# LayerNorm statistics computed on ScalarE instead of VectorE in a fused attention and recurrent-gate kernel

## The chip, the cores and the metric

One Trainium2 chip (trn2), all of its 8 cores, which run the same program on different rows and don't talk to each other. The metric is device time in microseconds (us) of the slowest core; the profile is of that core, here core 5.

## The reference

```python
# x: (8, 4096, 1024) fp32; 16 heads, hd = 64; layernorm over the last axis, eps = 1e-5
def attn(x):
    q, k, v = (x @ W.T).reshape(N, S, H, hd).transpose(0, 2, 1, 3)   # for Wq, Wk, Wv
    att = einsum('nqhd,nkhd->nhqk', q, k)       # q and k run over the 16 heads of one token
    att = softmax(att / sqrt(hd), axis=3)
    return einsum('nhqk,nkhd->nqhd', att, v).reshape(N, S, D) @ Wo.T + bo

def ffn(x):                                     # scan over the first axis, 8 steps
    step: f = sigmoid(xt @ wf.T + c @ uf.T + bf); i = sigmoid(xt @ wi.T + c @ ui.T + bi)
          g = tanh(xt @ wc.T + c @ uc.T + bc);    c = f * c + i * g
    return tanh(x @ wo.T + c_final @ uo.T + bo)

x = x + layernorm(attn(layernorm(x)))
x = x + layernorm(ffn(layernorm(x)))
```

Attention goes over the heads of one token, so a 128x128 score tile packs 8 tokens by 16 heads, and masked rows of qst and kst cut it to its blocks.

## The kernel before

Each core holds 512 tokens of each of the 8 batches. Every engine has one queue in program order, written out by hand; `P("vector", f)` appends f to VectorE's queue, and semaphores in `Chan` objects order the engines. `f_...` are the pieces, named as in the code. SBUF tiles of 128 rows by 1024 columns are double-buffered (`buf`, `zbuf`); the four row statistics s1, s2, mean and rstd have one column for each buffer (`sl`).

**Projection tiles** (from L1486, four for each batch): POOL loads 128 rows of x into xin (`f_load`, L1500), once tile t-2 has been applied. Then come the statistics (`ln_stats`), the apply on VectorE (L1516, xln_sb), 8 transposes on TensorE (L1531), a copy (L1541), 48 matmuls for q, k and v (L1555) with VectorE's evictions (L1570), and transposes of q and k with four strided copies on VectorE into qst and kst (L1618). All of this is one chain; the next tile's row sum stands in VectorE's queue behind the last copy into kst.

**Attention groups** (16 for each batch): POOL loads vst (L1644), TensorE makes the scores (L1660), ScalarE the exp (L1672), TensorE the product with v (L1692), VectorE evicts and normalises (L1708, L1741), SP stores.

**P2** (`emit_P2`, from L1358) is the output projection of the batch before, one row tile after every fourth group: POOL loads zin, TensorE transposes, 16 matmuls (L1421), VectorE adds the bias in two halves (L1432, zb), statistics, then on VectorE apply (L1460) and residual (L1463), and POOL stores x1 (L1472). POOL's queue holds that store ahead of the next loads of vst or xin. The last batch's four row tiles come at the end.

**Stage of transposes** (32 tiles, after a barrier): x1 is loaded into xin (L1858), statistics, apply (L1881), transposes (L1893), copy (L1902), and a spill to xt_scr on SP (L1910). VectorE's first piece waits for the load of the gate weights as well (L1867).

**Scan** (L1969 to L2002): no LayerNorm in it. **Output matmuls** (32 row tiles): POOL loads gat from xt_scr (L2041), two groups of 17 matmuls (L2062, L2069, L2075), ScalarE evicts each through tanh into h (L2084), VectorE sums h and its squares (`f_hstat`, L2094, L2095). **Last stage**: apply and residual on VectorE, loads and stores on POOL.

`ln_stats` (L57) queues on VectorE a row sum (L61), a sum of squares as accumulator of a product (L62), and four operations on one column for mean and variance (L65 to L70); then on ScalarE Ln and Exp for rstd (L76, L78).

Of the kernel before, what the change touches and what calls it, by code (L numbers as in the profile page):

```python
# [9 lines left out]
AF = mybir.ActivationFunctionType  # L10
AL = mybir.AluOpType
AX = mybir.AxisListType.X

D = 1024
# [5 lines left out]
EPS = 1e-5  # L20
# [36 lines left out]
def ln_stats(P, ch_sum, ch_rst, xi, sq_junk, sl, s1, s2, mean, var, msq,  # L57
             rstd, epst, width):
    def f_sums(v, xi=xi, sl=sl):
        v.drain()  # L60
        v.reduce_sum(s1[:, sl], xi, axis=AX)  # L61
        v.scalar_tensor_tensor(sq_junk, xi, 1.0, xi, AL.mult, AL.mult,  # L62
                               accum_out=s2[:, sl])
        v.drain()  # L64
        v.tensor_scalar_mul(mean[:, sl], s1[:, sl], 1.0 / width)  # L65
        v.scalar_tensor_tensor(msq[:, sl], s1[:, sl], 1.0 / (width * width),
                               s1[:, sl], AL.mult, AL.mult)
        v.tensor_scalar_mul(var[:, sl], s2[:, sl], 1.0 / width)
        v.drain()
        ch_sum.inc(v.tensor_sub(var[:, sl], var[:, sl], msq[:, sl]))  # L70
    P("vector", f_sums)
    ch_sum.bump()

    def f_rstd(sc, sl=sl, sm=ch_sum.n):
        sc.wait_ge(ch_sum.sem, sm)
        sc.activation(msq[:, sl], var[:, sl], AF.Ln, bias=epst)  # L76
        sc.drain()
        ch_rst.inc(sc.activation(rstd[:, sl], msq[:, sl], AF.Exp, scale=-0.5))  # L78
    P("scalar", f_rstd)
    ch_rst.bump()  # L80

def build_attn_program(trunc="full"):
# [172 lines left out]
    for n in range(B):  # L257
        for tt in range(NTIL):
# [17 lines left out]
            def f_prewait(v, chx=chx, xd=chx.n):  # L276
                v.wait_ge(chx.sem, xd)
            P("vector", f_prewait)
            ln_stats(P, ch_sum, ch_rst, xi, sqj[:], sl, s1, s2, mean, var,
                     msq, rstd, epst[:], D)  # L280

# [877 lines left out]
def build_fused_program():  # L1159
# [54 lines left out]
    sqj = sb("sqj", [128, D], BF16)  # L1214
# [6 lines left out]
    epst = sb("epst", [128, 1], F32)  # L1221
    s1 = sb("s1", [128, 2], F32)
    s2 = sb("s2", [128, 2], F32)
    mean = sb("mean", [128, 2], F32)
    var = sb("var", [128, 2], F32)
    msq = sb("msq", [128, 2], F32)
    rlc = sb("rlc", [128, 4], F32)
    rstd = sb("rstd", [128, 2], F32)
# [10 lines left out]
    def c(name, step=1):  # L1239
        ch = Chan(st, nc, name, step)  # L1240
        _chans.append(ch)
        return ch
    ch_xd = (c("xd0", 16), c("xd1", 16))
    ch_cd = c("cd", 16)
    ch_sum = c("sum")
    ch_rst = c("rst")
# [21 lines left out]
    ch_zev = c("zev")  # L1268
# [9 lines left out]
    def tr_slot():  # L1278
        b = _trs[0] % 2
        _trs[0] += 1  # L1280
        return b

    P = Plan()
# [74 lines left out]
    def emit_P2(n, rt, ODS_DONE):  # L1358
# [5 lines left out]
        zbt = zb[:, zbuf * D:(zbuf + 1) * D]  # L1364
        ot_ = x1t[:, zbuf * D:(zbuf + 1) * D]
        sl = slice(zbuf, zbuf + 1)
# [45 lines left out]
        for fc in range(2):  # L1412
# [17 lines left out]
            def f_zev(v, zbt=zbt, fc=fc, psp=psp, zc=ch_z.n):  # L1430
# [6 lines left out]
            ch_zev.bump()  # L1437
            psfree[fc] = ch_zev.n

        ln_stats(P, ch_sum, ch_rst, zbt, sqj[:], sl, s1, s2, mean,  # L1440
                 var, msq, rstd, epst[:], D)

        def f_xl(s, n=n, rt=rt, zbuf=zbuf, chx=ch_xd[zbuf],
                 need=(ch_vfree.n - 1)):
# [41 lines left out]
    for n in range(B):  # L1486
        for tt in range(NTIL):
            gti = n * NTIL + tt
            buf = gti % 2
            xi = xin[:, buf * D:(buf + 1) * D]  # L1490
            xl = xln_sb[:, buf * D:(buf + 1) * D]
            xt = xlnT_t[:, buf * 1024:(buf + 1) * 1024]
            sl = slice(buf, buf + 1)
            chx = ch_xd[buf]

            def f_load(s, n=n, tt=tt, gti=gti, xi=xi, chx=chx,
                       need=ch_vfree.n - 1):
                if gti >= 2:
                    s.wait_ge(ch_vfree.sem, need)
                chx.inc(s.dma_start(  # L1500
                    out=xi, in_=x[n, tt * 128:(tt + 1) * 128, :]))
            P("gpsimd", f_load)
            chx.bump()

            def f_prewait(v, chx=chx, xd=chx.n):
                v.wait_ge(chx.sem, xd)
            P("vector", f_prewait)
            ln_stats(P, ch_sum, ch_rst, xi, sqj[:], sl, s1, s2, mean, var,
                     msq, rstd, epst[:], D)

            def f_apply(v, xi=xi, xl=xl, sl=sl, rs=ch_rst.n,
                        trneed=(tr_hist[gti - 2] if gti >= 2 else None)):
                v.wait_ge(ch_rst.sem, rs)
                if trneed:
                    v.wait_ge(trneed[0].sem, trneed[1])
                ch_xln.inc(v.tensor_scalar(xl, xi, mean[:, sl], rstd[:, sl],  # L1516
                                           AL.subtract, AL.mult))
                ch_vfree.inc(v.drain())
# [20 lines left out]
            def f_trev(v, xt=xt, trb=trb, trc=ch_trx[trb].n):  # L1539
                v.wait_ge(ch_trx[trb].sem, trc)  # L1540
                ch_trevx[trb].inc(v.tensor_copy(xt, ps_trx[trb][:]))  # L1541
# [85 lines left out]
        for grp in range(NPK // 4):  # L1627
# [139 lines left out]
            if grp % 4 == 3 and _p2prev is not None:  # L1767
                emit_P2(_p2prev[0], grp // 4, _p2prev[1])
# [34 lines left out]
    hmean = sb("hmean", [128, 32], F32)  # L1803
    hvar = sb("hvar", [128, 32], F32)
# [12 lines left out]
    ch_hev = c("hev")  # L1817
    ch_hst = c("hst")
# [25 lines left out]
    for tt in range(NT2):  # L1844
        buf = tt % 2
        xi = xin[:, buf * D:(buf + 1) * D]
        xl = xln_sb[:, buf * D:(buf + 1) * D]
        sl = slice(buf, buf + 1)
        chx = ch_xd[buf]

        def f_load(s, tt=tt, xi=xi, chx=chx, need=ch_vfree.n - 1,
                   asto=A_STO):
            if tt < 2:
                s.wait_ge(ch_sto[0].sem, asto[0])
                s.wait_ge(ch_sto[1].sem, asto[1])
            else:
                s.wait_ge(ch_vfree.sem, need)
            chx.inc(s.dma_start(out=xi, in_=x1[tt * 128:(tt + 1) * 128, :]))  # L1858
        P("gpsimd", f_load)
        chx.bump()  # L1860

        def f_pre(v, tt=tt, chx=chx, xd=chx.n, fc_=FCONSTS):
            v.wait_ge(chx.sem, xd)
            if tt == 0:
                v.wait_ge(ch_cd.sem, fc_)
                v.drain()
                v.memset(onesf[:], 1.0)  # L1867
                v.memset(onesr2[:], 1.0)
        P("vector", f_pre)
        ln_stats(P, ch_sum, ch_rst, xi, sqj[:], sl, s1, s2, mean, var, msq,  # L1870
                 rstd, epst[:], D)

        def f_apply(v, xi=xi, xl=xl, sl=sl, rs=ch_rst.n,
                    trneed=(ftr_hist[tt - 2] if tt >= 2 else None),
                    spneed=(ftrd_hist[tt - 2] if tt >= 2 else None)):
            v.wait_ge(ch_rst.sem, rs)
            if trneed:
                v.wait_ge(trneed[0].sem, trneed[1])
            if spneed:
                v.wait_ge(spneed[0].sem, spneed[1])  # L1880
            ch_xln.inc(v.tensor_scalar(xl, xi, mean[:, sl], rstd[:, sl],  # L1881
                                       AL.subtract, AL.mult))
            ch_vfree.inc(v.drain())  # L1883
        P("vector", f_apply)
        ch_xln.bump()
        ch_vfree.bump()

        trb = tr_slot()
        def f_tr(t, xl=xl, trb=trb, xc=ch_xln.n, tev=ch_trevx[trb].n):
            t.wait_ge(ch_xln.sem, xc)  # L1890
            t.wait_ge(ch_trevx[trb].sem, tev)
            for ft in range(8):
                inst = t.transpose(ps_trx[trb][:, ft * 128:(ft + 1) * 128],  # L1893
                                   xl[:, ft * 128:(ft + 1) * 128], ident_sb[:])
            ch_trx[trb].inc(inst)
        P("tensor", f_tr)
        ch_trx[trb].bump()
        ftr_hist.append((ch_trx[trb], ch_trx[trb].n))

        def f_trev(v, buf=buf, trb=trb, trc=ch_trx[trb].n):  # L1900
            v.wait_ge(ch_trx[trb].sem, trc)
            ch_trevx[trb].inc(v.tensor_copy(xln_sb[:, buf * D:(buf + 1) * D],  # L1902
                                            ps_trx[trb][:]))
        P("vector", f_trev)
        ch_trevx[trb].bump()
        TRE = (ch_trevx[trb], ch_trevx[trb].n)

        def f_sp(s, tt=tt, buf=buf, cht=ch_trd[buf], tev=TRE):
            s.wait_ge(tev[0].sem, tev[1])
            cht.inc(s.dma_start(  # L1910
                out=xt_scr[:, tt * 128:(tt + 1) * 128].rearrange(
                    "(ft p) r -> p ft r", p=128),
                in_=xln_sb[:, buf * D:(buf + 1) * D].rearrange(
                    "p (ft r) -> p ft r", ft=8)))
        P("sync", f_sp)
        ch_trd[buf].bump()
        ftrd_hist.append((ch_trd[buf], ch_trd[buf].n))
# [114 lines left out]
    for rt in range(NT2):  # L2032
# [54 lines left out]
            P("scalar", f_hev)  # L2087
            ch_hev.bump()

        def f_hstat(v, rt=rt, he=ch_hev.n):  # L2090
            v.wait_ge(ch_hev.sem, he)
            v.drain()
            hrow = h_view(rt)
            v.reduce_sum(hmean[:, rt:rt + 1], hrow, axis=AX)  # L2094
            ch_hst.inc(v.scalar_tensor_tensor(  # L2095
                sqj[:], hrow, 1.0, hrow, AL.mult, AL.mult,
                accum_out=hvar[:, rt:rt + 1]))
        P("vector", f_hstat)
        ch_hst.bump()
    HSTAT = ch_hst.n  # L2100

# [20 lines left out]
    for rt in range(NT2):  # L2122
        buf = rt % 2
        xi = xin[:, buf * D:(buf + 1) * D]
# [116 lines left out]
```

## Time and profile before

| | us |
|---|---|
| two runs | 3761.22 and 3872.25, median 3816.74 |
| profiled execution | 3762.4 |
| span of its slowest core (5) | 3760.9 |
| spans of all cores | 3723.7 to 3760.9 |

| engine | busy us | share of the span |
|---|---|---|
| TensorE, matmuls | 1961.3 | 52% |
| VectorE | 1283.5 | 34% |
| POOL | 332.8 | 9% |
| ScalarE | 298.7 | 8% |

Busy time of an engine leaves out its waits. The granted clock of TensorE is given as a share of 2.4 GHz: 0.50 is 1.2 GHz, 1.00 is 2.4 GHz. The chain of work that ended last is followed back from the last instruction, at each step to what released it.

### The profile page before, as it was taken

Reading aid. Unit: us, or ns where it says so; the run is one execution under the profiler, and the core shown is the slowest. Engines: PE = TensorE matmul, PEld = TensorE weight load, DVE = VectorE, ACT = ScalarE, POOL = GpSimd, SP = SyncE. Lnnn points to the kernel's source line nnn. Section 1 sums busy time; section 2 is a strip of 40 time slices with the busy share of each in tenths; the row PEclk is TensorE's granted clock in tenths of the full one; section 3 lists DMA queues with packets and bytes.
Section 4 is the critical chain, followed back from the end, with each engine's and each line's share of the span. In section 5 each row is a group of like instructions: output and inputs, shape, how many; then the busy total and the mean of one; then the engine's idle time right before and its main releaser. Section 6 shows DMA issues by size and latency. Waiting matters only on the chain.

```text
span 3760.9 us, 31847 instructions; the slowest of 8 cores (3723.7 to 3760.9 us)
## 1 busy us (share of the span) xinstructions
PE 1961.3 (52%) x9540; PEld 916.2 (24%) x9540; DVE 1283.5 (34%) x2426; ACT 298.7 (8%) x585; POOL 332.8 (9%) x510
## 2 busy tenths in 40 slices
PE   2545445454454453553543101199999996988000
PEld 0222122222222221221221001144444442333000
DVE  1444344343343443443433236511221121222222
ACT  0000000000000000000000000011111111111000
POOL 0010100101101002011011100000000000010111
PEclk9757566576575675765765655599999998999555
DMA  6011111211202102112012474300000003111333
GB/s 112 19 39 28 47 47 29 51 37 41 58 19 52 51 23 57 36 39 57 20 45 59 86 143 116 113 1 12 12 12 12 12 12 51 28 31 31 117 117 117
DMA packets 167404, 186.97 MB, mean 50 GB/s; under 512 B 109886, under 2 KB 122174, under 8 KB 167230
## 3 DMA queue, kind: packets, MB, share of 16 engines
q0 software_dynamic: 53456, 151.38, 15.4%
q1 hardware_dynamic: 113792, 33.57, 3.7%
q8 instruction: 91, 1.49, 0.2%
q14 instruction: 65, 0.53, 0.0%
HBM read 151.68 MB, written 58.72 MB: 56 GB/s over the span
## 4 chain that ended last, share of the span: by engine, by line
PE 50%; DVE 19%; DMA 9%; issue 9%; DVEq 5%; another core or an unknown queue 4%; ACT 4%; POOL 1%; ACTq 0%; POOLq 0%; SPq 0%
PE ps_p L1555 11%; PE ps_a L1969 9%; PE ps_a L1975 9%; DMA xin<-x 5%; PE ps_p L1421 5%; DVE s L61 3%; PE ps_p L2062 3%; DVEq L64 3%; PE ps_p L2069 3%; PE ps_a L1660 2%; DVE otn L1708 2%; DVE qst L1618 2%; DVE kst L1618 2%; DMA vst<-v_scr 2%
## 5 line engine op out<-in xcount | busy, mean ns | idle before, releaser
L1999 DVE TENSOR_TENSOR cT<-cT,gat 128x512 f32<-128x512 f32 x64 | 44.3, 692 | 578.4 <-ACT gat L1989 578.4
L1692 PE MATMUL ps_ot<-pt_sb,vst 128*65 128x128 bf16 x256 | 64.2, 287 | 285.6 <-DMA vst<-v_scr 238.5
L1421 PE MATMUL ps_p<-wo_sb,zlT_t 128*128 128x512 bf16 x512 | 181.6, 532 | 48.5 <-DVE zlT_t L1407 48.5
L1555 PE MATMUL ps_p<-wq_sb,xlnT_t 128*128 128x512 bf16 x512 | 185.4, 541 | 33.7 <-DVE xlnT_t L1541 33.7
L1989 ACT ACTIVATE gat<-ps_a,biases 128x512 f32<-128x512 f32 x192 | 132.0, 687 | 583.0 <-PE ps_a L1975 582.9
L1644 POOL DMA_DIRECT2D vst<-v_scr x128 | 96.1, 753 | 886.7 <-DMA v_scr<-vtok 582.2
L1969 PE MATMUL ps_a<-xtT_sl,wq_sb 128*128 128x512 bf16 x512 | 133.6, 408 | 49.4 <-DVE zb L1952 34.4
L2062 PE MATMUL ps_p<-qst,gat 128*128 128x512 bf16 x512 | 122.9, 383 | 58.2 <-DMA gat<-xt_scr 34.8
L76 ACT ACTIVATE msq<-var,epst 128x1 f32<-128x1 f32 x96 | 28.3, 295 | 1521.2 <-DVE var L70 1521.0
L1672 ACT ACTIVATE pt_sb<-ps_a 128x512 bf16<-128x512 f32 x128 | 76.1, 594 | 708.3 <-PE ps_a L1660 708.3
L1975 PE MATMUL ps_a<-zb,wk_sb 128*128 128x512 bf16 x512 | 125.8, 390 | 0.0
L1660 PE MATMUL ps_a<-qst,kst 73*128 73x128 bf16 x512 | 111.7, 258 | 19.4 <-DVEq L1620 19.0
L2069 PE MATMUL ps_p<-kst,zb 128*128 128x512 bf16 x512 | 121.2, 380 | 0.0
L1975 PE MATMUL ps_a<-zb,wo_sb 128*128 128x512 bf16 x512 | 121.0, 379 | 0.0
L1969 PE MATMUL ps_a<-xtT_sl,wv_sb 128*128 128x512 bf16 x512 | 121.0, 379 | 0.0
L1975 PE MATMUL ps_a<-zb,kst 128*128 128x512 bf16 x512 | 121.0, 379 | 0.0
L1969 PE MATMUL ps_a<-xtT_sl,qst 128*128 128x512 bf16 x512 | 120.9, 379 | 0.0
L1708 DVE CAST otn<-ps_ot 65x512 bf16<-65x512 f32 x64 | 44.0, 687 | 219.9 <-PE ps_ot L1692 219.9
L1893 PE MATMUL ps_tr<-ident_sb,xln_sb 128*128 128x128 bf16 x128 | 16.2, 306 | 191.7 <-DVEq L1883 104.2
L1555 PE MATMUL ps_p<-wk_sb,xlnT_t 128*128 128x512 bf16 x512 | 115.7, 379 | 0.0
L1555 PE MATMUL ps_p<-wv_sb,xlnT_t 128*128 128x512 bf16 x512 | 115.7, 379 | 0.0
L1692 PEld LDWEIGHTS ps_ot<-pt_sb,vst 128*65 128x65 bf16 x256 | 33.5, 131 | 316.2 <-issue 297.3
(156 smaller groups left out, 2724.0 us busy)
## 6 DMA issues: line engine op xcount, KB each, us to landing
xin<-x POOLq DMA_DIRECT2D x96, 512.0 KB, 4.7
xin<-xr POOLq DMA_DIRECT2D x32, 512.0 KB, 4.2
x<-x1t POOLq DMA_DIRECT2D x32, 512.0 KB, 3.1
out<-x1t POOLq DMA_DIRECT2D x32, 512.0 KB, 3.3
v_scr<-vtok SPq DMA_DIRECT2D x32, 256.0 KB, 2.0
vst<-v_scr POOLq DMA_DIRECT2D x128, 64.0 KB, 2.6
od<-orow SPq DMA_DIRECT2D x128, 64.0 KB, 1.8
zin<-od POOLq DMA_DIRECT2D x128, 64.0 KB, 3.3
```

What stands on the lines that cost most here:

```text
L61: v.reduce_sum(s1[:, sl], xi, axis=AX)
L64: v.drain()
L1421: inst = t.matmul(psp[:, :], zt_[:, ft * 128:(ft + 1) * 128], wo_sb[:, ft * D + fc * 512: ft * D + (fc + 1) * 512], start=(ft == 0), stop= ...
L1555: inst = t.matmul(psp[:, :], xt[:, ft * 128:(ft + 1) * 128], w_sb_[:, ft * D + fc * 512: ft * D + (fc + 1) * 512], start=(ft == 0), stop=( ...
L1618: inst = v.tensor_copy(out_ap, in_ap)
L1660: inst = t.matmul(ps_a[:, acol:acol + 128], kst[0:73, pk * 128:(pk + 1) * 128], qst[0:73, pk * 128:(pk + 1) * 128], start=True, stop=True)
L1708: ch_nrm.inc(v.tensor_copy(otn[0:65, obuf * 512:(obuf + 1) * 512], psot[0:65, :]))
L1969: t.matmul(ps_a[:, pg * 512:(pg + 1) * 512], w_sb[wn][:, ft * D + mt * 128: ft * D + mt * 128 + 128], xtT_sl[:, buf * 4096 + ft * 512: buf ...
L1975: inst = t.matmul(ps_a[:, pg * 512:(pg + 1) * 512], w_sb[un][:, m2 * D + mt * 128: m2 * D + mt * 128 + 128], cT_bf[:, m2 * 512:(m2 + 1) * ...
L1989: ch_gev.inc(sc.activation(gat[:, gi * 512:(gi + 1) * 512], ps_a[:, pg * 512:(pg + 1) * 512], func, bias=biases[:, bcol + mt:bcol + mt + 1]))
L2062: t.matmul(psh[:, :], xr_sl[:, buf * 1024 + ft * 128: buf * 1024 + (ft + 1) * 128], wo_sl[:, fc * 4096 + ft * 512: fc * 4096 + (ft + 1) * ...
L2069: t.matmul(psh[:, :], cT_bf[:, m2 * 512 + bsl * 128: m2 * 512 + (bsl + 1) * 128], uo_sl[:, fc * 4096 + m2 * 512: fc * 4096 + (m2 + 1) * 51 ...
```

## The change

`ln_stats_sc` takes the place of `ln_stats` at its three calls of the program that runs: in the projection tiles, in P2 and in the stage of transposes. It puts the whole of the statistics into ScalarE's queue as one piece, which waits for the semaphore of the load (projection tiles, stage of transposes) or of the second bias addition (P2): Square over the 1024 columns with accumulator s2, Copy over them with accumulator s1, the mean, the squared mean, EPS minus the squared mean, Ln with scale 1/width and that as its bias, Exp. VectorE's pieces with the sums, and in the projection tiles its wait for the load, are gone. In the output matmuls the two sums over h move to ScalarE in the same way (`f_hstat`).

```diff
+def ln_stats_sc(P, ch_rst, xi, sq_junk, sl, s1, s2, mean, msq, rstd, width,
+                wait=None):
+    def f_stat(sc, xi=xi, sl=sl, wait=wait):
+        if wait is not None:
+            sc.wait_ge(wait[0].sem, wait[1])
+        sc.activation(sq_junk, xi, AF.Square, accum_out=s2[:, sl])
+        sc.drain()
+        sc.activation(sq_junk, xi, AF.Copy, accum_out=s1[:, sl])
+        sc.drain()
+        sc.mul(mean[:, sl], s1[:, sl], 1.0 / width)
+        sc.activation(msq[:, sl], s1[:, sl], AF.Square, scale=1.0 / width)
+        sc.drain()
+        sc.activation(msq[:, sl], msq[:, sl], AF.Copy, scale=-1.0, bias=EPS)
+        sc.drain()
+        sc.activation(rstd[:, sl], s2[:, sl], AF.Ln, scale=1.0 / width,
+                      bias=msq[:, sl])
+        sc.drain()
+        ch_rst.inc(sc.activation(rstd[:, sl], rstd[:, sl], AF.Exp, scale=-0.5))
+    P("scalar", f_stat)
     ch_rst.bump()
@@ emit_P2
-        ln_stats(P, ch_sum, ch_rst, zbt, sqj[:], sl, s1, s2, mean,
-                 var, msq, rstd, epst[:], D)
+        ln_stats_sc(P, ch_rst, zbt, sqj[:], sl, s1, s2, mean,
+                    msq, rstd, D, wait=(ch_zev, ch_zev.n))
@@ projection tiles
-            def f_prewait(v, chx=chx, xd=chx.n):
-                v.wait_ge(chx.sem, xd)
-            P("vector", f_prewait)
-            ln_stats(P, ch_sum, ch_rst, xi, sqj[:], sl, s1, s2, mean, var,
-                     msq, rstd, epst[:], D)
+            ln_stats_sc(P, ch_rst, xi, sqj[:], sl, s1, s2, mean,
+                        msq, rstd, D, wait=(chx, chx.n))
@@ stage of transposes
-        ln_stats(P, ch_sum, ch_rst, xi, sqj[:], sl, s1, s2, mean, var, msq,
-                 rstd, epst[:], D)
+        ln_stats_sc(P, ch_rst, xi, sqj[:], sl, s1, s2, mean,
+                    msq, rstd, D, wait=(chx, chx.n))
@@ output matmuls
-        def f_hstat(v, rt=rt, he=ch_hev.n):
-            v.wait_ge(ch_hev.sem, he)
-            v.drain()
+        def f_hstat(sc, rt=rt, he=ch_hev.n):
+            sc.wait_ge(ch_hev.sem, he)
+            sc.drain()
             hrow = h_view(rt)
-            v.reduce_sum(hmean[:, rt:rt + 1], hrow, axis=AX)
-            ch_hst.inc(v.scalar_tensor_tensor(
-                sqj[:], hrow, 1.0, hrow, AL.mult, AL.mult,
-                accum_out=hvar[:, rt:rt + 1]))
-        P("vector", f_hstat)
+            sc.activation(sqj[:], hrow, AF.Square,
+                          accum_out=hvar[:, rt:rt + 1])
+            sc.drain()
+            ch_hst.inc(sc.activation(sqj[:], hrow, AF.Copy,
+                                     accum_out=hmean[:, rt:rt + 1]))
+        P("scalar", f_hstat)
```

## Rows read from the trace of the kernel before

**Rows 1.** The page's chain that ended last, share of the span by engine

```profile
PE 50%; DVE 19%; DMA 9%; issue 9%; DVEq 5%; another core or an unknown queue 4%; ACT 4%; POOL 1%; ACTq 0%; POOLq 0%; SPq 0%
```

**Rows 2.** Stretches: us, busy of PE, PEld, DVE, ACT, POOL, clock, DMA share, GB/s

```profile
443.00:698.00 255.00, 124.13 (x638) 60.47 (x638) 105.65 (x215) 12.74 (x32) 28.96 (x44) 0.65 0.15 41
2210.00:2434.00 224.00, 32.37 (x256) 24.78 (x256) 141.82 (x299) 15.92 (x64) 15.87 (x30) 0.50 0.38 109
3166.00:3477.00 311.00, 251.68 (x1088) 101.52 (x1088) 77.02 (x102) 40.05 (x67) 30.02 (x34) 0.95 0.20 42
```

**Rows 3.** Timeline, projection tiles 0 and 1: start, length, engine, operation [idle before, releaser]

```profile
508.88 0.53 POOL L1500 DMA_DIRECT2D xin<-x  x1 [9.74 <-DVEq L1518]
...
531.30 1.22 DVE L61 TENSOR_REDUCE s<-xin 128x1 f32<-128x1024 f32 x1 [0.26 <-issue]
...
534.36 0.29 ACT L76 ACTIVATE msq<-var,epst 128x1 f32<-128x1 f32 x1 [27.06 <-DVE var L70]
534.72 0.20 ACT L78 ACTIVATE rstd<-msq 128x1 f32<-128x1 f32 x1
535.10 0.81 DVE L1516 TENSOR_SCALAR xln_sb<-xin,mean,rstd 128x1024 bf16<-128x1024 f32 x1 [0.83 <-ACT rstd L78]
```

**Rows 4.** Timeline, one row tile of P2 and the group behind it

```profile
455.00 0.69 DVE L1432 TENSOR_TENSOR zb<-ps_p,bo_bc 128x512 f32<-128x512 f32 x1 [2.22 <-PE ps_p L1421]
...
459.64 0.81 DVE L1460 TENSOR_SCALAR zb<-zb,mean,rstd 128x1024 f32<-128x1024 f32 x1 [0.90 <-ACT rstd L78]
...
462.95 1.51 POOL L1644 DMA_DIRECT2D vst<-v_scr  x2
...
466.43 0.98 PE L1692 MATMUL ps_ot<-pt_sb,vst 128*65 128x128 bf16 x4 [11.31 <-DMA vst<-v_scr]
```

**Rows 5.** Groups by line and form: count, busy us, mean ns, idle before, releasers

```profile
L1989 ACT ACTIVATE gat<-ps_a,biases 128x512 f32<-128x512 f32 x192 | 132.0, 687 | 583.0 <-PE ps_a L1975 582.9
L1672 ACT ACTIVATE pt_sb<-ps_a 128x512 bf16<-128x512 f32 x128 | 76.1, 594 | 708.3 <-PE ps_a L1660 708.3
L78 ACT ACTIVATE rstd<-msq 128x1 f32<-128x1 f32 x96 | 19.5, 203 | 6.5
L62 DVE DVE_READ_ACCUMULATOR sqj<-xin 128x1 f32 x64 | 5.2, 82 | 0.0
L1323 ACT ACT_TABLE_LOAD x1 | 1.3, 1283 | 63.3 <-PE ps_rl L1315 63.3
```

**Rows 6.** Timeline, ScalarE's first statistic

```profile
69.60 0.29 ACT L76 ACTIVATE msq<-var,epst 128x1 f32<-128x1 f32 x1 [0.17 <-issue]
```

**Rows 7.** The chain in order of time: start, length, two bursts of P2 in one batch

```profile
413.77 5.06 PE ps_p L1421 x16
...
448.42 6.49 PE ps_p L1421 x16
```

**Rows 8.** Stage of transposes: timeline, and the landing of line 1858's loads

```profile
2210.55 0.48 DVE L1867 MEMSET bo_bc<- 128x512 f32 x1 [91.88 <-DMA xin<-x]
...
2228.79 0.81 DVE L1881 TENSOR_SCALAR xln_sb<-xin,mean,rstd 128x1024 bf16<-128x1024 f32 x1 [0.90 <-ACT rstd L78]
2230.18 0.53 POOL L1858 DMA_DIRECT2D xin<-x  x1 [6.29 <-DVEq L1883]
...
2427.60 0.81 DVE L1881 TENSOR_SCALAR xln_sb<-xin,mean,rstd 128x1024 bf16<-128x1024 f32 x1 [0.90 <-ACT rstd L78]
...
DMA to landing us min/median/max: 3.6/3.8/78.5
```

**Rows 9.** DMA issues: line or queue, count, KB each, median us to landing

```profile
xin<-x POOLq DMA_DIRECT2D x96, 512.0 KB, 4.7
xt_scr<-xln_sb SPq DMA_DIRECT2D x32, 256.0 KB, 3.1
```

**Rows 10.** Timeline of the output matmuls: one load and the group that waits for it

```profile
3231.72 0.88 POOL L2041 DMA_DIRECT2D gat<-xt_scr  x1 [7.88 <-PE ps_p L2075]
...
3236.09 1.89 PE L2062 MATMUL ps_p<-qst,gat 128*128 128x512 bf16 x8 [1.03 <-ACT wq_sb L2084]
```

More of the change, by code:

```diff
@@ L79, in ln_stats @@
     P("scalar", f_rstd)
+    ch_rst.bump()
+def ln_stats_sc(P, ch_rst, xi, sq_junk, sl, s1, s2, mean, msq, rstd, width,
[17 more added lines that the diff above has]
+    P("scalar", f_stat)
     ch_rst.bump()
```

## The prediction

> **What bounds the kernel now.** I read the chain that ended last first: TensorE holds half of it, VectorE 19%, transfers 9% [rows 1]. A mean over the span says little here, so the stages come next, as stretches [rows 2]. One batch of the attention (about 256 us each, eight of them) has TensorE busy for 124 of 255 us at a granted clock of 0.65: no engine is full, and the batch is a string of waits. The stage of transposes before the scan (2210 to 2434) has VectorE busy for 142 of 224 us and TensorE for 32. The stage of the output matmuls (3166 to 3477) has TensorE busy for 252 of 311 us, ScalarE for 40. The scan and the last stage hold none of the changed lines. Then the timeline, for what a LayerNorm costs where it stands.
>
> In a projection tile VectorE starts the row sum at 531.30, having been idle for 0.26 us behind the last copy into kst, and the apply at 535.10 [rows 3]: 3.80 us in which VectorE works on the statistics or waits for ScalarE, and TensorE waits for both. In the output projection of a batch (P2) the second bias addition ends at 455.69 and the apply starts at 459.64: 3.95 us. Behind it stand the store of x1 and, in POOL's queue, the next load of vst (462.95), for which TensorE waits until 466.43 [rows 4].
>
> **The change, part by part.**
>
> *The price on ScalarE.* No ScalarE operation on 1024 columns is in the trace. Its 128x512 exp takes 594 ns and its 128x1 exp 203 ns [rows 5]: 0.765 ns a column, so 986 ns for 1024. Two of 512 end to end would be 1188, or 1374 in the slower form with a bias tile (687); these are the bounds, and I take 1.05 us, near the low one, since a fixed part is paid once. Reading the accumulator out costs VectorE 82 ns, and a whole small ScalarE operation costs 203: I take 0.2, between 0 and 0.3. A drained step adds 0.07: the Ln at 534.36 lasts 0.29 and its Exp starts at 534.72 [rows 3]. So: Square and Copy 2 x (1.05 + 0.2 + 0.07) = 2.64; the mean and the squared mean, overlapping, 0.38; the Copy with EPS 0.27; Ln 0.36; Exp 0.20; until VectorE starts 0.25. That is 4.1, with the semaphore ahead of it S = 4.2 us; by the bounds 3.6 and 5.0. On VectorE it was 3.8 to 3.95. The statistics get no shorter: about 0.3 us more wherever they are waited for. All of the gain must come from overlap.
>
> The Trainium skill speaks against such a move (ScalarE: Activation LUTs, Rules for kernel authors): adds and multiplies belong on VectorE, the faster one per element. The row sum here takes VectorE 1.22 us for 1024 fp32 columns [rows 3], more than my 1.05; the page's cost formula (186 ns + 0.833 ns a column) gives ScalarE an estimated 1.04 us. For fp32 reductions this trace doesn't bear the rule out.
>
> *Projection tiles.* ScalarE has nothing there between the statistics of two tiles. Tiles 0 and 1 are loaded together; the load of tile 2 is issued at 508.88, as soon as tile 0 is applied, and lands 4.7 us later [rows 3, 9], while VectorE comes to tile 1 only at 531.30. So 4.2 us of ScalarE fit in ahead, and the apply starts where the row sum started. That is 3.80 us for tiles 1 to 3 of eight batches, and for tile 0 of the second batch, whose loads stand behind no store of x1: 25 x 3.80 = -95. If this cover is gone, each costs 0.4 instead. Late next are VectorE's four strided copies and the transposes, unchanged.
>
> Tile 0 of batches 2 to 7 waits for its load, so it pays 4.2 - 3.8 = 0.4: +3. The first tile of all waits for ScalarE, which turns to it at 69.60 [rows 6]; today Ln and Exp remain from there, 0.7 us, afterwards all 4.2: +4.
>
> *P2, 32 times.* ScalarE waits for the second addition as VectorE did. S stands on the path to the store and to the load of vst: 32 x 0.3 = +10; by the bounds of S -10 and +35. Queued behind the waiting ScalarE is the exp of the next group. It already waits for Ln and Exp today, and its consumer starts at 466.43 with vst, so it costs nothing. POOL's queue behind the store moves by the same 0.3.
>
> *The clock.* After its pauses TensorE restarts at 1.2 GHz. A burst of 16 matmuls took 5.06 us at one place and 6.49 at another of the same batch [rows 7], by how long it ran before the clock rose to 2.4 GHz, and moved starts move this. I take no net change, and a quarter of the 1.43 us between the two, 0.35, either way for 64 bursts: +-22. That the pause ahead of a projection gets shorter I count as no gain in clock: the light work with transposes on both sides of it stays.
>
> *The stage of transposes, 32 tiles.* Today VectorE is the loop: from 2228.79 (apply of tile 2) to 2427.60 (tile 31), 29 intervals of 6.86 us [rows 8]. Without the 3.8 us of statistics 3.1 are left for apply, transposes and copy. The new loop goes over two tiles of one buffer: apply 0.81, to POOL's issue 0.58 (2229.60 to 2230.18), landing, ScalarE 0.1 + 4.2, next apply. The landing is 3.8 us in the median of this line [rows 8], 4.7 over all loads of xin [rows 9]; at a faster pace it overlaps more with the spill, so I take 4.2. Sum 9.9 us for two tiles, 4.95 each. ScalarE alone needs about 4.1 a tile: close, but not the bound. The loop over the spill, 3.1 + 3.1 [rows 9], is 6.2 us for two tiles: not the bound. The weights release VectorE at 2210.55 and the statistics of two tiles are done by then, so tile 0 is applied at 2211.2, tile 30 at 2211.2 + 15 x 9.9 = 2359.7, tile 31 about 4 us later, against 2427.60: -64. With landing 3.8 and S 3.6 it is -79, with 4.7 and 5.0 it is -43.
>
> *Output matmuls.* The loop there is the transfer: issue at 3231.72, TensorE starts at 3236.09 [rows 10], and the next issue waits for that group. ScalarE gets 32 x 2.6 us beside its 40 of 311, between two evictions that are half a row tile (9.7 us) apart: hidden, 0; if the cover were gone, at most 1 us a row tile, +32. Only the last row tile's statistics are exposed, +0.3, not counted.
>
> **Sum.** -95 + 3 + 4 + 10 - 64 = -142 us. The profiled execution took 3762.4 us (span 3760.9), so 3620. The median shown, 3816.74, is that of 3761.22 and 3872.25 and stands 54 us above the profiled execution.
>
> **The rivals.**
>
> *A: table switching (it ends slower).* ScalarE's first table load, 1283 ns, stands ahead of the copy of line 1323 and serves every Ln and Exp of the attention [rows 5]. So Copy is in one set with Ln and Exp; Square is nowhere in this trace. If it is outside, each statistic carries two loads, x = 2.6 us by the row. P2 and the 7 exposed first tiles pay 39x, the loop of the stage of transposes x for two tiles, 16x in all; the projections still hide theirs: -142 + 55x, which is +1 at 2.6: 3763. With a flush as long as each load x is 5.2: +144, 3906. It decides for slower by over 2% from x = 4. The Trainium skill (ScalarE: Activation LUTs, What ACT_TABLE_LOAD costs) gives an estimated 2.66 us a switch with its drain, so an estimated 3913 by its price; it also says that cheap functions are filler in every set, and does not list square there. Chance 0.10, of it 0.06 for slower.
>
> *B: ScalarE dearer than taken.* S = 5.0: 39 x 0.8 = +31, and the stage saves 51 instead of 64: 3664. For it speaks that no such row is there. Chance 0.17.
>
> *C: the stage of transposes stays bound by transfers.* With a landing of 7 us the loop is 12.7 for two tiles and saves 22: 3662. Against it: the load lands in 3.8 us with a spill in flight already. Chance 0.10.
>
> *D: no overlap in the projections*, by a wait that I overlooked: -142 + 95 + 10 = -37: 3725. Against it: ScalarE's queue holds nothing else there, and the new wait names the load alone. Chance 0.05.
>
> **How the numbers follow.** My forecast has 0.58, with 3570 to 3665 as its own range (below: P2 20, the clock 22, the stage 15, not all together; above about the same). The range: low 3570; above it takes in B and C and the 54 us by which a median can stand over the profiled execution: 3730. From 3687 up a result is within 2%, about what a measurement of this kernel can tell from no change. Faster 0.83 (forecast, B and most of C), within 2% 0.11 (D, the cheap half of A, the rest of C), slower 0.06 (the dear half of A).
>
> **What would show it.** VectorE's row sums of 1024 gone; ScalarE forms of 128x1024 at about 1.05 us; no more table loads than today. In a projection tile the apply starts about 0.3 us after the last copy into kst. In P2 4.1 to 4.4 us from the second addition to the apply. The stage of transposes at 4.9 us a tile, its end near 2434 - 78 - 64 = 2292. The scan, the output matmuls and the last stage as long as before. The forecast is wrong if there are table loads in the hundreds, ScalarE passes of over 1.4 us, or a VectorE that waits for rstd in the projections.

## The result and the profile after

The kernel after ran in 3603.54 us (median of 9 runs, 3592.21 to 3691.65); the kernel before, on the same chip, in 3762.37 us (median of 8, 3752.50 to 3910.02). The ratio is 0.958, with a 95% interval from 0.956 to 0.960: 159 us faster. The forecast was 3620. A few executions of either kernel, such as the one of 3691.65 us, are some per cent longer with a lower granted clock on the cores of one die, and the ratio leaves them out.

The page of the profiled execution, with span, busy time and the chain that ended last, to be held against [rows 1]:

```profile
span 3591.7 us, 31970 instructions; the slowest of 8 cores (3571.9 to 3591.7 us)
...
PE 1965.7 (55%) x9540; PEld 917.2 (26%) x9540; DVE 938.0 (26%) x1658; ACT 638.6 (18%) x1385; POOL 333.0 (9%) x510
...
PE 51%; DVE 15%; DMA 12%; issue 8%; ACT 7%; another core or an unknown queue 4%; DVEq 1%; POOL 1%; ACTq 1%; POOLq 0%; SPq 0%
```

VectorE lost 345 us of work and ScalarE gained 340, so the kernel does as much as before. VectorE fell from 19% of the chain to 15% and its queue from 5% to 1%; ScalarE rose from 4% to 7%.

The three stretches that answer to [rows 2], in the same columns (a batch of the attention, the stage of transposes, the output matmuls):

```profile
440.00:686.00 246.00, 124.92 (x640) 60.79 (x640) 84.22 (x165) 35.56 (x88) 28.95 (x44) 0.65 0.17 43
2130.00:2280.00 150.00, 32.38 (x256) 24.78 (x256) 50.75 (x71) 100.75 (x279) 15.87 (x30) 0.50 0.58 161
3007.00:3318.00 311.00, 251.67 (x1093) 101.62 (x1092) 4.28 (x4) 109.55 (x188) 34.22 (x37) 0.95 0.20 43
```

A batch takes 246 us instead of 256. In a stretch of 311 us the output matmuls have the same 252 us of TensorE work as before, although ScalarE has 110 us of work there instead of 40. The bounds of the stretches are round; the lengths of the stages are in the table below. The granted clock is the same in each stretch: 0.65, 0.50 (all at the lower level, 1.2 GHz) and 0.95.

By the stage, from starts of one line of each, over all eight cores:

| | before | after | difference | predicted |
|---|---|---|---|---|
| last apply of P2 (end of the attention) | 2109.5 to 2118.0 | 2028.0 to 2035.3 | -81 in the mean | -78 |
| stage of transposes, first to last apply | 212.6 | 142.8 to 146.7 | -68 | -60 |
| output matmuls, first to last start of the first line | 274.3 to 278.2 | 274.6 to 277.5 | -0.6 in the mean | 0 |
| last stage, first to last apply | 246.3 to 275.0 | 247.3 to 260.0 | -3.5 in the mean | 0 |

The -60 is the predicted -64 without the 3.7 us by which the stage was to start earlier. The spans differ by 155 us in the mean of the cores, and by 169 (3760.9 and 3591.7) for the slowest. Of these 169 the last stage is 18: it took 275.0 us on core 5 before and 256.7 on core 6 after. Experiment 4 asks whether that is the change's.

**Statistics on ScalarE.** Groups by form of the kernel after (count, busy us and mean ns, idle before and its releasers):

```profile
L90 ACT ACTIVATE sqj<-xin 128x1024 bf16<-128x1024 f32 x64 | 67.6, 1056 | 4.3
L88 ACT ACTIVATE sqj<-xin 128x1024 bf16<-128x1024 f32 x64 | 67.3, 1052 | 361.3 <-DMA xin<-x 361.1 <-issue 0.2
L88 ACT ACTIVATION_READ_ACCUMULATOR sqj<-xin 128x1 f32 x64 | 11.9, 186 | 0.0
...
L1345 ACT ACT_TABLE_LOAD x1 | 1.3, 1283 | 62.3 <-PE ps_rl L1337 62.3
L2008 ACT ACT_TABLE_LOAD x1 | 1.3, 1283 | 19.9 <-PE ps_a L1994 19.9
L2135 ACT ACT_TABLE_LOAD x1 | 1.3, 1283 | 0.8 <-DVE hvar L2129 0.8
```

Square (L88) and Copy (L90) take 1.05 us each and the read of the accumulator 0.19, as taken (1.05 and 0.2). In the projections and the stage of transposes ScalarE waits for loads only. There are three table loads in the whole program, at the attention's first copy, at the scan and at the last stage, and the kernel before has the same three (one in [rows 5], the others here):

```profile
L1989 ACT ACT_TABLE_LOAD x1 | 1.3, 1283 | 17.9 <-PE ps_a L1975 17.9
L2115 ACT ACT_TABLE_LOAD x1 | 1.3, 1283 | 3.3 <-DVE hvar L2109 3.3
```

Square causes none, neither beside Ln and Exp nor, in the output matmuls, beside Tanh. That is rival A gone.

**A projection tile.** Timeline of the kernel after, what answers to [rows 3], tiles 0 and 1 of a batch:

```profile
486.08 0.20 ACT L100 ACTIVATE rstd<-rstd 128x1 f32<-128x1 f32 x1
486.19 1.04 ACT L88 ACTIVATE sqj<-xin 128x1024 bf16<-128x1024 f32 x1
486.46 0.81 DVE L1535 TENSOR_SCALAR xln_sb<-xin,mean,rstd 128x1024 bf16<-128x1024 f32 x1 [11.11 <-ACT rstd L100]
487.87 0.53 POOL L1522 DMA_DIRECT2D xin<-x  x1 [10.37 <-DVEq L1537]
...
489.60 0.20 ACT L100 ACTIVATE rstd<-rstd 128x1 f32<-128x1 f32 x1
...
508.46 1.22 DVE L1637 COPY kst<-ps_tr 64x1024 bf16<-64x1024 bf16 x1 [0.20 <-issue]
509.96 0.81 DVE L1535 TENSOR_SCALAR xln_sb<-xin,mean,rstd 128x1024 bf16<-128x1024 f32 x1 [0.28 <-issue]
```

ScalarE goes from tile 0's statistics straight to tile 1's and has them at 489.80, 20 us before VectorE comes for them. The apply starts 0.28 us behind the last copy into kst, where the row sum started before, and has no releaser but VectorE's own issue. That is the forecast's step as it was written. The last copy into kst in the kernel before, which [rows 3] leave out, shows the gap as it was: it ended at 531.05, and the apply came at 535.10, 4.05 us later.

```profile
529.83 1.22 DVE L1618 COPY kst<-ps_tr 64x1024 bf16<-64x1024 bf16 x1 [0.20 <-issue]
```

**P2.** What answers to [rows 4]:

```profile
433.31 0.69 DVE L1454 TENSOR_TENSOR zb<-ps_p,bo_bc 128x512 f32<-128x512 f32 x1 [2.18 <-PE ps_p L1443]
434.09 1.06 ACT L88 ACTIVATE sqj<-zb 128x1024 bf16<-128x1024 f32 x1 [12.62 <-DVE zb L1454]
435.06 0.19 ACT L88 ACTIVATION_READ_ACCUMULATOR sqj<-zb 128x1 f32 x1
435.31 1.06 ACT L90 ACTIVATE sqj<-zb 128x1024 bf16<-128x1024 f32 x1
...
437.97 0.81 DVE L1482 TENSOR_SCALAR zb<-zb,mean,rstd 128x1024 f32<-128x1024 f32 x1 [3.97 <-ACT rstd L100]
...
441.30 1.51 POOL L1663 DMA_DIRECT2D vst<-v_scr  x2
```

From the addition's end (434.00) to the apply: 3.97 us, against 3.95 before. VectorE waits the whole time, where it used to work. Over all 256 of them on the eight cores the mean is 3.98 us against 3.97 before.

**The stage of transposes.** Tiles 0 and 1, against [rows 8]:

```profile
2126.26 1.06 ACT L88 ACTIVATE sqj<-xin 128x1024 bf16<-128x1024 f32 x1 [93.24 <-DMA xin<-x]
2126.54 0.48 DVE L1886 MEMSET bo_bc<- 128x512 f32 x1 [91.15 <-DMA xin<-x]
2130.00 0.81 DVE L1900 TENSOR_SCALAR xln_sb<-xin,mean,rstd 128x1024 bf16<-128x1024 f32 x1 [2.85 <-ACT rstd L100]
2131.39 0.53 POOL L1877 DMA_DIRECT2D xin<-x  x1 [81.08 <-DVEq L1902]
...
2135.82 1.06 ACT L88 ACTIVATE sqj<-xin 128x1024 bf16<-128x1024 f32 x1 [2.39 <-DMA xin<-x]
...
2139.69 0.81 DVE L1900 TENSOR_SCALAR xln_sb<-xin,mean,rstd 128x1024 bf16<-128x1024 f32 x1 [3.29 <-ACT rstd L100]
```

The loop is the one that was written down: apply 0.81, issue 0.58 later (2130.81 to 2131.39), landing, statistics, next apply of the same buffer. Both waits in it are to be seen: ScalarE for the load, VectorE for ScalarE.

### The profile page after: what moved, and what is told of

Its sections match the earlier page's. It is cut to its first block, busy times and chain, and to the rows that moved or that the text cites. A ratio compares the mean times of both kernels' runs of the same rounds, so it can differ in the third digit from the quotient of the medians.

```text
span 3591.7 us, 31970 instructions; the slowest of 8 cores (3571.9 to 3591.7 us)
## 1 busy us (share of the span) xinstructions
PE 1965.7 (55%) x9540; PEld 917.2 (26%) x9540; DVE 938.0 (26%) x1658; ACT 638.6 (18%) x1385; POOL 333.0 (9%) x510
## 4 chain that ended last, share of the span: by engine, by line
PE 51%; DVE 15%; DMA 12%; issue 8%; ACT 7%; another core or an unknown queue 4%; DVEq 1%; POOL 1%; ACTq 1%; POOLq 0%; SPq 0%
PE ps_p L1574 11%; PE ps_a L1988 10%; PE ps_a L1994 9%; DMA xin<-x 7%; PE ps_p L1443 5%; PE ps_p L2081 3%; PE ps_p L2088 3%; PE ps_a L1679 3%; DVE otn L1727 2%; DVE kst L1637 2%; DVE qst L1637 2%; DMA vst<-v_scr 2%; PE ps_ot L1711 2%; PE ps_rl L1711 2%
## 5 line engine op out<-in xcount | busy, mean ns | idle before, releaser
L88 ACT ACTIVATE sqj<-xin 128x1024 bf16<-128x1024 f32 x64 | 67.3, 1052 | 361.3 <-DMA xin<-x 361.1
L88 ACT ACTIVATE sqj<-zb 128x1024 bf16<-128x1024 f32 x32 | 33.8, 1056 | 405.5 <-DVE zb L1454 405.5
```

The costliest lines, as they stand in the source:

```text
L88: sc.activation(sq_junk, xi, AF.Square, accum_out=s2[:, sl])
```

## The experiments

The theory: the gain is overlap alone. 3.8 us a projection tile leave the path, the stage of transposes goes over to a loop of load and statistics, and P2 and the output matmuls change nothing. The rivals: part of the 169 us is elsewhere (clock, last stage), the projection gain needs no cover, or ScalarE is not what bounds the new loop.

### 1 to 4. One part of the change at a time

Each is the kernel before with one of the four edits. The form of the first, for the projection tiles; the other three change their calls alike:

```diff
-            def f_prewait(v, chx=chx, xd=chx.n):
-                v.wait_ge(chx.sem, xd)
-            P("vector", f_prewait)
-            ln_stats(P, ch_sum, ch_rst, xi, sqj[:], sl, s1, s2, mean, var,
-                     msq, rstd, epst[:], D)
+            ln_stats_sc(P, ch_rst, xi, sqj[:], sl, s1, s2, mean,
+                        msq, rstd, D, wait=(chx, chx.n))
```

Projection tiles alone:

> Only the projection tiles' statistics go to ScalarE; P2, the stage of transposes and the sums over h stay on VectorE. Theory (overlap): 25 tiles lose 3.8 us each less what the clock takes back (about 0.3), the first tile of all pays 3: -80 to -90 us, ratio 0.977. Rival (VectorE's relief as such speeds transfers and the last stage too, and the parts share the gain): less than -60 here, and the missing part in e2_p2 and e4_hstat.

P2 alone:

> Only P2's statistics go to ScalarE. Theory: they are waited for at either place. In the profile after, VectorE idles 3.98 us between the second addition and the apply, against 3.95 before, so 32 x 0.03 = +1 us and not the +10 of the prediction: within 5 us of the kernel before. Rival (relief of VectorE): -10 us or more.

The stage of transposes alone:

> Only the stage of transposes goes to ScalarE. Theory: the loop over a load becomes the bound, 4.6 us a tile instead of 6.86, and everything ahead of it and behind it stays: -68 to -72 us, ratio 0.981. Rival: over -80, because transfers of the last stage gain as well.

The sums over h in the output matmuls alone:

> Only the sums over h go to ScalarE. Theory: hidden behind the transfer that bounds the output matmuls, 0 us, within 4 us of before. Rival: the 10 to 20 us by which the last stage of the slowest core is shorter in the profile after come from here: -10 or more, with a last stage of under 250 us on all cores.

| edit alone | ratio to before | 95% interval | us | its stage |
|---|---|---|---|---|
| projection tiles | 0.9758 | 0.9728 to 0.9788 | -91 | attention ends at 2025 to 2036 |
| P2 | 0.9996 | 0.9969 to 1.0023 | -2 | attention ends at 2112 to 2124 |
| stage of transposes | 0.9796 | 0.9741 to 0.9851 | -77 | 143.3 to 147.2 us |
| sums over h | 1.0007 | 0.9979 to 1.0036 | +3 | output matmuls unchanged |
| sum of the four | 0.9557 | | -167 | |
| all four (the change) | 0.9578 | 0.9558 to 0.9597 | -159 | |

Two of the four carry the gain; the other two are no change that these runs can tell from none. They add up within the intervals, so nothing large lies between them. The projection tiles' -91 is at the edge of the expected -80 to -90; the attention ends 81 us earlier there in the mean of the cores. The stage of transposes came out somewhat above the expected -68 to -72, with the stage itself at the length it has in the whole change; the interval of the ratio, about 20 us either way, holds both, and the spans of the profiled execution are 72 us shorter in the mean of the cores.

The last stage: with the sums over h on ScalarE it still took 267 and 270 us on cores 4 and 5 in the profiled execution, so that edit did not shorten it. It stayed at 250 to 254 us on all cores in experiments 3, 6 and 8, and reached 269 to 280 on cores 2 and 3 or 4 and 5 in 1, 2, 5 and 7 (in 2 also 265 on cores 0 and 1), with kernels whose code of this stage is the same. What grows is the wait for loads. In the last stage of the profile before, VectorE waits for those of xin for 209.2 us on core 5 and 174.7 on core 0:

```profile
DVE x1t L2141 <- DMA xin<-x: 209.2, 31, 7.2
...
DVE x1t L2141 <- DMA xin<-x: 174.7, 30, 6.1
```

So the 18 us between the two profiled executions go with the execution rather than with an edit, as far as one profile of each kernel can tell. Why the loads land late on two neighbouring cores at a time isn't settled.

### 5. The cover of the projections taken away

The kernel after, with ScalarE made to wait for the last copy into kst before it starts the statistics of the next tile. What is computed is the same.

```diff
+            def f_stkwait(sc, stk=ch_stk.n):
+                if stk:
+                    sc.wait_ge(ch_stk.sem, stk)
+            P("scalar", f_stkwait)
             ln_stats_sc(P, ch_rst, xi, sqj[:], sl, s1, s2, mean,
                         msq, rstd, D, wait=(chx, chx.n))
```

> The changed kernel, but ScalarE's statistic of a projection tile waits for the last copy into kst of the tile before, so that it stands where VectorE's stood. Theory (all of the projection tiles' gain is overlap): 24 tiles get a wait of 0.1 + 3.88 us instead of 0.28, 24 x 3.7 = +89 us over the changed kernel, less what the clock gives back (about 0.3 a tile): 3675 to 3695. Rival (VectorE's relief itself gains): less than +50.

Of the first set of runs one time can be compared, 3695.99 us, at the upper end of the expected 3675 to 3695. The second set has an expectation of its own:

> The kernel of e5_cover once more, since one comparison alone was undisturbed there. Theory: the projection tiles give back all of their gain, +80 to +90 us over the changed kernel, 3680 to 3695 us. Rival: under +50.

Measured: 0.9819 (0.9726 to 0.9911), that is 0.0241 x 3762 = 91 us above the kernel after, by the interval some 35 either way. The trace is sharper: the attention ends at 2111 to 2117, where it ended before the change, 82 us later in the mean than in the kernel after. Timeline at a tile's boundary:

```profile
529.71 1.22 DVE L1641 COPY kst<-ps_tr 64x1024 bf16<-64x1024 bf16 x1 [0.20 <-issue]
531.12 1.06 ACT L88 ACTIVATE sqj<-xin 128x1024 bf16<-128x1024 f32 x1 [23.35 <-DVEq L1643]
...
534.93 0.81 DVE L1539 TENSOR_SCALAR xln_sb<-xin,mean,rstd 128x1024 bf16<-128x1024 f32 x1 [4.00 <-ACT rstd L100]
```

The statistics are still on ScalarE and VectorE has as little work as in the kernel after, yet the apply starts 4.00 us behind the copy, as it did before (531.05 to 535.10, [rows 3]). The interval between two applies of a batch is back as well, 27.41 us (27.39 before the change). So of the projections' gain none comes from less work on VectorE: all of it is that the statistics run ahead.

### 6. Four buffers in the stage of transposes

The kernel after, with the two buffers of x1t, idle in this stage, lent to xin, and four columns in s1, s2, mean and rstd: loads run four tiles ahead instead of two.

```diff
-        xi = xin[:, buf * D:(buf + 1) * D]
+        b4 = tt % 4
+        xsrc = xin if b4 < 2 else x1t
+        xi = xsrc[:, buf * D:(buf + 1) * D]
...
-        sl = slice(buf, buf + 1)
-        chx = ch_xd[buf]
-
-        def f_load(s, tt=tt, xi=xi, chx=chx, need=ch_vfree.n - 1,
+        sl = slice(b4, b4 + 1)
+        chx = ch_xd4[b4]
+
+        def f_load(s, tt=tt, xi=xi, chx=chx, need=ch_vfree.n - 3,
...
-            if tt < 2:
+            if tt < 4:
```

> The changed kernel, but in the stage of transposes the tiles of x1 are loaded into four buffers (x1t lends two), so a load waits for the apply of four tiles ago. Theory (the loop over two buffers, apply + issue + landing + statistic = 9.2 us for two tiles, is the bound): the bound moves to ScalarE's own 3.9 to 4.1 us a tile, against 4.62 now: -16 to -22 us. Rival C (transfers themselves are the bound): no gain, within 4 us. Rival (ScalarE is the bound already): no gain either, with ScalarE idle for under 0.1 us a tile.

Measured: 3576.02 us, 0.9465 (0.9419 to 0.9512), and the stage 110.0 to 110.4 us on every core, 3.55 a tile: 34 us less than with two buffers, where 16 to 22 were expected. The whole time fell by 43 us by the ratios (with some 20 either way), by 28 by the medians, and by 33 in the mean span of the profiled executions. The stage as a stretch, and ScalarE and VectorE in it:

```profile
2134.00:2245.00 111.00, 31.36 (x248) 23.99 (x248) 47.23 (x63) 98.57 (x279) 14.79 (x28) 0.50 0.78 205
```

```profile
2200.84 1.04 ACT L88 ACTIVATE sqj<-xin 128x1024 bf16<-128x1024 f32 x1
...
2204.36 1.04 ACT L88 ACTIVATE sqj<-xin 128x1024 bf16<-128x1024 f32 x1
...
2208.57 0.81 DVE L1903 TENSOR_SCALAR xln_sb<-xin,mean,rstd 128x1024 bf16<-128x1024 f32 x1 [1.00 <-DMA xt_scr<-xln_sb]
```

That it fell at all shows the loop of load and statistics as the bound of this stage in the kernel after. Where it fell to shows the next bound: ScalarE, busy for 98.6 of 111 us and without a pause between two tiles, one every 3.52 us (2200.84 to 2204.36). The expectation, and the "ScalarE alone needs about 4.1 a tile" of the prediction, counted the hand-over to VectorE (0.36 to 0.45 us) in ScalarE's own time; while VectorE takes the result, ScalarE is at the next tile. VectorE waits here and there for the spill of the tile before (2208.57), which is close to being the bound as well.

### 7. A forced change of table in P2

Rival A didn't happen, so its price was never seen. The kernel after, with a Sigmoid of one column ahead of each of the 32 statistics of P2; its result is not used.

```diff
+        def f_sw(sc, zc=ch_zev.n, sl=sl, zbt=zbt):
+            sc.wait_ge(ch_zev.sem, zc)
+            sc.activation(var[:, sl], zbt[:, 0:1], AF.Sigmoid)
+            sc.drain()
+        P("scalar", f_sw)
```

> The changed kernel, with one Sigmoid of one column ahead of each of P2's 32 statistics; the output is as before. It forces ScalarE to change its table and back: two loads of 1.28 us each on the path, and 0.27 us for the Sigmoid. Theory: the row's price is the whole price, 32 x 2.8 = +91 us, by the clock +-20. Rival (a flush as long as each load, as the Trainium skill has it in ScalarE: Activation LUTs, What ACT_TABLE_LOAD costs): 32 x 5.5 = +176 us.

Measured: 0.9827 (0.9762 to 0.9892), 94 us above the kernel after; the attention ends at 2114 to 2137. ScalarE and VectorE in one P2:

```profile
400.42 1.28 ACT L1464 ACT_TABLE_LOAD   x1 [11.61 <-DVE zb L1454]
401.71 0.20 ACT L1464 ACTIVATE var<-zb 128x1 f32<-128x1 f32 x1
...
405.09 1.28 ACT L97 ACT_TABLE_LOAD   x1
406.38 0.29 ACT L97 ACTIVATE rstd<-s,msq 128x1 f32<-128x1 f32 x1
...
407.12 0.81 DVE L1487 TENSOR_SCALAR zb<-zb,mean,rstd 128x1024 f32<-128x1024 f32 x1 [6.78 <-ACT rstd L100]
```

The operation behind a load starts as soon as the 1.28 us are over (401.71 and 406.38), and VectorE waits 6.78 us instead of 3.97: 2.81 more, twice 1.28 and the Sigmoid's 0.25. 32 x 2.81 = 90 of the 94 us, and the interval of the ratio, some 25 us either way, leaves the rival's 176 out. The Trainium skill (ScalarE: Activation LUTs, What ACT_TABLE_LOAD costs) has the same 1283 ns and adds a drain of 1380 ns to each switch; by that the wait would be an estimated 9.5 us, and these rows don't show it. Both loads stand here behind a wait or a `drain()` of ScalarE, so what a switch costs with operations still under way is not shown. With x = 2.6 rival A would have given +1 by the prediction's sum and not +144: its half "slower by over 2%" was not there to be had. The second load stands at Ln (L97), behind both passes: Square and Copy ran in Sigmoid's set as well.

### 8. P2's statistics split over both engines

P2 gained nothing because all the statistics wait for the second addition. In this version the additions carry the row sum as they go, ScalarE squares each half behind its addition, and VectorE does the four small steps (`f_small`: the mean and EPS + E[x^2] - mean^2 from hs1 and hs2); `f_ln` is Ln and Exp:

```diff
-                inst = v.tensor_add(zbt[:, fc * 512:(fc + 1) * 512],
-                                    psp[:, :],
-                                    bo_bc[:, fc * 512:(fc + 1) * 512])
+                inst = v.scalar_tensor_tensor(
+                    zbt[:, fc * 512:(fc + 1) * 512], psp[:, :], 1.0,
+                    bo_bc[:, fc * 512:(fc + 1) * 512], AL.mult, AL.add,
+                    accum_out=hs1[:, fc:fc + 1])
...
-        ln_stats_sc(P, ch_rst, zbt, sqj[:], sl, s1, s2, mean,
-                    msq, rstd, D, wait=(ch_zev, ch_zev.n))
+            def f_sqh(sc, zbt=zbt, fc=fc, ze=ch_zev.n):
+                sc.wait_ge(ch_zev.sem, ze)
+                ch_sum.inc(sc.activation(
+                    sqj[:, fc * 512:(fc + 1) * 512],
+                    zbt[:, fc * 512:(fc + 1) * 512], AF.Square,
+                    accum_out=hs2[:, fc:fc + 1]))
+            P("scalar", f_sqh)
...
+        P("vector", f_small)
...
+        P("scalar", f_ln)
```

> The changed kernel, but P2's statistic is split over both engines: VectorE's two bias additions accumulate the row sum as they go, ScalarE squares each half behind its addition, VectorE makes mean and EPS + E[x^2] - mean^2 on one column, ScalarE Ln and Exp. Left on the path: half a Square 0.65 + 0.19, drain 0.07, semaphores 0.2, Ln 0.36, Exp 0.2, to VectorE 0.25: 2.0 us against 3.98. Theory (P2's statistic is exposed in full, POOL's store and load of vst behind it): 32 x 2.0 = -63 us, by the clock +-20. Rival (the load of vst or something else hides part of it): under -30.

Measured: 3546.78 us, 0.9402 (0.9355 to 0.9449), 66 us under the kernel after by the ratios (57 by the medians); the attention ends at 1974 to 1980, 55 us earlier. One P2:

```profile
429.08 0.69 DVE L1457 SCALAR_TENSOR_TENSOR zb<-ps_p,bo_bc 128x512 f32<-128x512 f32 x1 [1.93 <-PE ps_p L1446]
...
429.88 0.63 ACT L1468 ACTIVATE sqj<-zb 128x512 bf16<-128x512 f32 x1 [1.91 <-DVE zb L1457]
...
431.12 0.29 ACT L1495 ACTIVATE rstd<-hs,msq 128x1 f32<-128x1 f32 x1 [0.52 <-DVE msq L1488]
...
431.93 0.81 DVE L1520 TENSOR_SCALAR zb<-zb,mean,rstd 128x1024 f32<-128x1024 f32 x1 [0.90 <-ACT rstd L1498]
```

The addition takes the same 0.69 us with its accumulator as without, and only one 512-column pass is left behind it: 2.16 us from 429.77 to the apply in this one, 1.87 in the mean of all 256, instead of 3.98. 32 x 2.11 would be 67, and the attention ended 55 us earlier. The clock took back the 12 between them: the burst of 16 matmuls ahead of the additions got longer, from 5.69 to 6.15 us in the mean (196 bursts on eight cores in each profile), which comes to 14 us for some 30 of them. So P2's statistics stood on the path in full, and a shorter pause of TensorE gave a fifth of the gain back. Their length behind the second addition is what mattered; which engine did them did not (experiment 2).

### 9. Both together

Experiments 6 and 8 in one kernel.

> The changed kernel with the four buffers of e6_four and the split statistic of e8_split together. Theory: the two lie in different stages, so their gains add: by the profiles -34 us in the stage of transposes and -55 in the attention over the changed kernel, 3500 to 3515 us, ratio 0.931 to the kernel before. Rival: one stage waits for a resource that the other frees (transfers), and less than 70 us come.

Measured: 3523.49 us (3521.94 to 3524.59), 0.9374 (0.9355 to 0.9393), 80 us under the kernel after by the medians and 77 by the ratios, and the fastest of all. The expected 3500 to 3515 was missed by 8 us. Both stages came as expected (110.5 us on nearly every core; attention ended at 1974 to 1981), but the last stage took 272 to 278 us on cores 2 to 5 and 252 to 258 on the others. The spans of an early and a late core:

```profile
core 0: 3497.1 us, clock 0.727
...
core 3: 3520.4 us, clock 0.727
```

Between them lie 23 us, of which 19 are the last stage (252.3 and 271.7). This is the lateness by pairs of cores that experiment 4 left open, here on two pairs, and with four closely agreeing times it may belong to this kernel's own timing. No run tells.

## Why the prediction was right

**Projection tiles (-95 predicted).** Right in mechanism: shown by experiments 1 and 5. The exposed gap behind the last copy fell from 4.05 to 0.28 us, 3.77 a tile. The tile itself got only 3.52 shorter: over all 8 cores and 8 batches of four tiles the interval between two applies is 27.39 us before and 23.87 after. The missing 0.25 lies in TensorE's first 16 matmuls after the pause: in 112 such bursts, on four cores, they take 5.81 us in the mean before and 6.04 after. The records of the granted clock show why: it rose from 0.50 to 1.00 on average 4.5 us into the burst before and 5.0 after (198 bursts each, eight cores). In experiment 5, with the pause back, the burst is back at 5.8 as well. It is the term "no net change" of the clock, and its sign was against the gain: 25 x 0.25 = 6 us, inside the +-22. The first tile of all came 3 us later (72.3 to 73.4 against 69.3 to 70.8), where 4 were taken. The six tiles 0 that wait for their load were taken at 0.4 each and cost nothing: 3.81 us from the first pass to the apply against 3.79.

**P2 (+10 predicted).** The step was right and too dear: 3.97 against 3.95 us, so about +1. S had been taken as 4.2 and was 3.9 to 4.0. The small operations, Ln and Exp came as taken. The over-sized term is the two passes: 1.22 us from Square to Copy (434.09 to 435.31), not 1.05 + 0.2 + 0.07 = 1.32, because the read of the accumulator starts 0.09 before the pass ends. With its read a pass on ScalarE takes about as long as VectorE's row sum (1.22 us), so neither engine is clearly the faster one here. Projections and P2 together: -25 x 3.5 + 3 + 1 = -84, and -81 was measured; no run settles the 3 between them. That the predicted -78 came so near is partly luck: P2 (9 us) and the tiles 0 (2) were taken too dear, the clock (6) too cheap.

**The stage of transposes (-64 predicted, -69 measured).** The loop was right in every member: apply 0.81, issue 0.58, landing 3.9 in the median (taken 4.2), ScalarE and the hand-over 3.9 to 4.0 (taken 4.3), 9.3 for two tiles instead of 9.9, 4.65 a tile against the 4.95: 144.4 us from the first apply to the last, where the prediction's own steps give 152.5 (2211.2 to 2363.7). Against it stands a step that failed, a wait that was read wrongly: "The weights release VectorE at 2210.55 and the statistics of two tiles are done by then". They are not. In the row of the memset in [rows 8] the releaser named is the load of xin, not the weights; in the kernel after ScalarE starts on tile 0 at 2126.26, together with the memset, and the apply comes 3.5 us behind the memset instead of 0.7. The apply was 4.4 behind the memset before, so the head start was 1 us instead of 3.7. That cost 2.8 us, and the loop gave 8 more than summed.

**What was costed at nothing.** The output matmuls took 0 (experiment 4), the scan 0. The cover held: ScalarE has 110 us of work in 311 there.

**The rivals.** A (tables) fell with three table loads, the same as before. By its own sum, with the load's 1283 ns that experiment 7 shows, it would have eaten the gain and not more. That sum is too small in the stage of transposes: with x on top ScalarE's own 4.1 + x a tile is longer than (9.9 + x) / 2, so an estimate from the prediction's own terms is +15 at x = 2.6 and +200 at 5.2, and slower by 2% would begin near x = 3.4 and not 4. B (ScalarE dearer) fell: it was cheaper. C (a landing of 7 us) fell: it was 3.9. That the landing is part of the new loop was the forecast's own step, and experiment 6, which takes it out of the loop, gains 34 us. D (no overlap in the projections) is what experiment 5 builds: 82 us by the end of the attention and 91 by the ratios, where the prediction had 95 for it.

**The difference of 17 us** between 3620 and 3603.54: the slowest cores of the profiled executions (5 before, 6 after) differ by 169, 27 more than the 142. On them the stages of the change give 153, 11 more than summed (in the mean of the cores -81 - 69 = -150); the last stage gives 18, which goes with the execution; the rest took 2 longer. The median after stands 10 us above its profiled execution, and the one before at it, so 17 of the 27 are left. That the whole came out nearer than the profiled executions is the place of a median, not a merit of the sum.

## What to carry to other kernels

Moving statistics from a busy engine to an idle one gains nothing by itself: 3.97 us of ScalarE took the place of 3.95 of VectorE. Here it paid where the idle engine could start before the busy one came, so look for the earliest moment at which the input is there and for what stands ahead in the new engine's queue. Where the input itself comes last, split the work so that most of it runs with its producer, and after every such move write down the next loop, with its buffers: here it was load and statistics over two tiles of one buffer, and two idle buffers were worth another 34 us.

## What the runs showed that was not expected

- A sum accumulated by the bias addition costs its engine 0.08 us for the read of the accumulator and nothing in the addition (0.69 us with and without); the same on ScalarE costs 0.19 us.
- A switch of table on a ScalarE that had nothing under way cost 1.28 us and no more, with the next operation right behind it (experiment 7).
- A shorter pause of TensorE did not bring the clock up sooner: the first 16 matmuls of a projection took 0.23 us longer, and those of P2 0.45 in experiment 8.
- The last stage takes 246 to 280 us, mostly by pairs of cores (2 and 3, 4 and 5), in kernels that have the same code there, and the late cores wait longer for loads. Up to 28 us of the slowest core's time thus come from something that no experiment here touched; a gain of that size in one profiled execution is not to be credited to an edit.
